# Graph network kernel: one wait per batch on GpSimd, on a TensorE product, in all three edge passes

## The chip, the cores and the metric

The kernel runs on one core of one Trainium2 chip. The metric is device time in microseconds of one execution. Before the change, three timed runs took 8580.19, 8585.12 and 8589.28 us; their median is 8585.12 us.

## The reference, cut to what matters

Four graph layers run one after the other on 6250 nodes of 64 features and 206250 edges that are sorted by destination. After each, the node features are a layer norm of the old ones plus the layer's result.

```
L0 (mlp):   m = relu([x[src], x[dst], edge_attr_32] @ W1 + b1) @ W2 + b2 ; segment_sum(m, dst)
L1 (gatv2): g = leaky_relu(xl[src] + xr[dst] + edge_attr_16 @ W_e) ; logits = sum(g * att)
            softmax over the edges of one destination, out = segment_sum(alpha * xl[src]) ...
L2 (gat):   e = leaky_relu(s_src[src] + s_tgt[dst]) ; softmax ; segment_sum(attention * h[src])
L3 (mean):  segment_sum(x[src]) / counts
```

The first three gather a row of a node table for every edge (`x[src]`, `xl[src]`, `h[src]`). This gather is what the change touches.

## The kernel before, in words

L0, L1 and L2 are each run by `edge_pass` (L195), followed by a `dense` stage; L3 is a function of its own. The pass of L0 is called mlp, that of L1 gatv (in the program gatv2), that of L2 gat. gatv and gat are the *soft* passes, those with a softmax (`soft`, L197).

A pass walks over 231 batches (`NB`) of 7 tiles (`B`) of 128 edges. Each engine has its own program of steps, one per batch, and the programs are tied together by counting semaphores; `b.used(k)` is n + 1 - k for batch n, so `wait(eng, sem, b.used(k))` waits until batch n - k has passed the place that counts `sem`. A wait for a count of zero or less is not issued at all (`wait`, L138). SyncE, VectorE, ScalarE and TensorE run their steps in a loop with eight batches in its body and the first and last batches written out (`over_batches`, L144); GpSimd's program has all 231 batches written out.

What each engine does for a batch n:

- **GpSimd** (L459 to L473) waits, then issues 7 indirect DMAs (L470), one per tile, which gather 128 rows each from the node table into slot n mod 8 of the tile `G` (8 slots, `GQ`). It computes nothing else in this part of the pass.
- **SyncE** loads the edge's relative destinations (`rel`, L361), edge attributes (L367), 4 of the 7 windows of the destination table (L374 and L167 through `load_windows`) two batches ahead, and stores results. ScalarE's queue loads the other 3 windows.
- **VectorE** makes one-hot matrices of the destinations for the next batch (`one_hots`, L489), adds the gathered rows to TensorE's product z (`add_gathered`, L510, counting `z_added`), makes the matrix of equal destinations (L496) and, in the soft passes, the prefix maxima (L526, L530), the difference from the maximum of the batch two behind (L547, which waits for TensorE's turned maxima, `max_turned`) and the weighted messages (L554, counting `msg_ready`).
- **ScalarE** applies the nonlinearity to z plus the gathered rows (L717 or L713), exponentials, copies sums and the "build" blocks out of PSUM (L705, L734).
- **TensorE**, in this order in a step i: the first group of a build block (L865), `make_z(i + 1)` (L794 to L813, counting `z_made`), in the soft passes `turn_max` and `turn_logits` (L821, L828), the sums by destination (L846), in mlp the degree counts (L855), and the second group of the build block. `make_z(b)` itself waits for `z_added` of batch b - 2 in mlp, and for `act_done` of b - 2 and `msg_ready` of b - 3 in the soft passes, so that only two z tiles in PSUM are in use.

What holds GpSimd back before the change:

- In mlp: `z_added` of batch n - 8, that is, the slot of `G` is free again. GpSimd runs eight batches ahead.
- In the soft passes two waits: `msg_ready` of batch n - 8 (the slot is free), and `z_made` of batch n - 1, which keeps GpSimd no more than about one batch ahead. `msg_ready` is a count of VectorE's, `z_made` one of TensorE's. For the first eight batches of a soft pass the wait for `msg_ready` would be for a count of zero or less and is not there.

Of the kernel before, what the change touches and what calls it, by code (L numbers as in the profile page):

```python
# [32 lines left out]
GQ = 8  # L33
# [104 lines left out]
def wait(eng, sem, count):  # L138

    if not isinstance(count, int) or count > 0:  # L140
        eng.wait_ge(sem, count)
# [53 lines left out]
def edge_pass(nc, L, S, hist):  # L195

    soft = L.heads > 0  # L197
# [6 lines left out]
    with ctx:  # L204
# [6 lines left out]
        def sem(name):  # L211
            return ctx.enter_context(nc.semaphore(f"{L.name}_{name}"))
# [84 lines left out]
        sums_made = sem("sums_made")  # L297
        sums_copied = sem("sums_copied")
        z_added = sem("z_added")
        act_done = sem("act_done")  # L300
        if L.window:
            win_in = [sem(f"win_in{q}") for q in range(Q)]
            hot_made = sem("hot_made")
            z_made = sem("z_made")
        if ax:
            attr_in = [sem(f"attr_in{q}") for q in range(Q)]
        if soft:
# [10 lines left out]
            msg_ready = sem("msg_ready")  # L318
# [37 lines left out]
        def _(sp):  # L356
# [54 lines left out]
            def load_steps(n):  # L411

                for h, (k, m) in enumerate(THIRDS):
                    if n == LOAD_AT[h]:
                        sp.wait_ge(step_stored, 16)
                        if h:
                            sp.wait_ge(tiles_hot, h)
                            sp.wait_ge(groups_made, k)
                        sp.dma_start(tile_of[:, 0:m, :].rearrange("p b e -> p (b e)"),
                                     S["step_of"][k * P:(k + m) * P].unsqueeze(0).to_broadcast([P, m * P])  # L420
                                     ).then_inc(tiles_in, 16)
                    g = (n - LOAD_AT[h]) * LOADS
                    w = min(LOADS, m - g)
                    if g >= 0 and w > 0:
                        _, firsts = nc.values_load_multi_w_load_instructions(
                            first_tile[0:1, k + g:k + g + w], engines=[sp.engine], min_val=0, max_val=NTP - P,
                            skip_runtime_bounds_check_because="the least of a tile's number and the last window's")
                        for j, first in enumerate(firsts):
                            sp.dma_start(step_rows[:, g + j, :], S["tile_rows"][bass.ds(first, P), :]
                                         ).then_inc(rows_in, 16)  # L430
# [26 lines left out]

        @block.gpsimd
        def _(pool):  # L459
            freed = {"mlp": z_added, "gatv2": None, "gat": None, "mean": sums_made}[L.name]  # L460
            freed = freed or msg_ready

            for n in range(NB):
                b = Batch(0, n)
                wait(pool, freed, b.used(GQ))
                if soft:
                    wait(pool, z_made, b.used(1))
                for j in range(b.tiles()):
                    t = n * B + j
                    pool.indirect_dma_start(  # L470
                        out=G[:, b.gq, j * L.gathered:(j + 1) * L.gathered], out_offset=None, in_=L.gather_table,
                        in_offset=bass.IndirectOffsetOnAxis(ap=S["src_cols"][:, t:t + 1], axis=0)
                    ).then_inc(gathered[b.gq], 16)  # L473
            pool.wait_ge(written, 16 * (4 + 2 * HEADS * hist))
            for r in range(RA):
                pool.wait_ge(back_copied, sum(1 for _, first, _ in backs if first <= r))
                pool.indirect_dma_start(
                    out=S["C_" + L.name], out_offset=bass.IndirectOffsetOnAxis(ap=S["carry_row"][:, r:r + 1], axis=0),
                    in_=carried_rows[:, r, :], in_offset=None, bounds_check=NP - 1, oob_is_err=False
                ).then_inc(S["scattered"], 16)  # L480
            pool.wait_ge(S["scattered"], 16 * (RB * L.index + RA))

        @block.vector
        def _(dve):
# [118 lines left out]
            def carry_tails(n):  # L603
                v, through = nc.vector, S["through"]
                if soft and n == turns_at:
                    dve.wait_ge(tails_in, 16 * len(PASS_TAILS))
                    for c, (_, k) in enumerate(PASS_TAILS):
                        last = widen(v, L, wide[0:k, c, :, :], tails[0:k, c, :, :])
                    last.then_inc(wide_made, 1)
# [91 lines left out]
        def _(act):  # L701
# [36 lines left out]
            def copy_tails(n):  # L738
                if 0 <= n - turns_at < len(turns):
                    to, _, t0, k, j0, m = turns[n - turns_at]  # L740
                    act.wait_ge(turned, n - turns_at + 1)
                    act.activation(to[:, t0:t0 + k * B].rearrange("f (n b) -> f b n", b=B)[:, j0:j0 + m, :],
                                   build_ps[0:M, 0:m * P].rearrange("f (b n) -> f b n", b=m)[:, :, 0:k], ACT.Copy
                                   ).then_inc(turns_copied, 1)
                if soft and n == scan_at + 1:
                    act.wait_ge(tops_shifted, 1)
                    act.activation(tail_max, tail_max, ACT.Exp)
                    act.activation(fade[:, 1:TA], fade[:, 1:TA], ACT.Exp).then_inc(faded, 1)
                if 0 <= n - backs_at < len(backs):
                    a, r, m = backs[n - backs_at]  # L750
                    act.wait_ge(back, n - backs_at + 1)
                    part, to = (slice(0, M), slice(0, M)) if a is state else (slice(D, M), slice(M, L.row))
                    act.activation(carried_rows[:, r:r + m, to],
                                   build_ps[:, 0:m * P].rearrange("p (r f) -> p r f", r=m)[:, :, part], ACT.Copy
                                   ).then_inc(back_copied, 1)
# [1532 lines left out]
```

## Time and profile before

| | |
|---|---|
| median of 3 runs | 8585.12 us (8580.19 to 8589.28) |
| the profiled execution's own time | 8576.33 us |
| its span in the trace | 8574.6 us |
| mean granted TensorE clock | 0.546 |
| TensorE matmuls busy | 5662.1 us (66% of the span) |
| TensorE weight loads busy | 4975.2 us (58%) |
| VectorE busy | 4808.3 us (56%) |
| ScalarE busy | 1444.1 us (17%) |
| GpSimd busy | 4949.5 us (58%) |
| gathers of the three passes (L470) | 1612 in each; first starts 87.4, 2889.4 and 5578.2 us, last starts 2671.7, 5367.0 and 8044.3 us |

Busy time counts an instruction from its start to its end on the engine; for a DMA issued by GpSimd that is the time that GpSimd works on it, not the transfer. Matmuls overlap, and their ends are modelled. Idle time is shown in front of the instruction that ended it, with what released it where the semaphores tell; "issue" means that nothing was waited for that the profile shows, "remote" that the releaser could not be named. A releaser that is a DMA of an earlier stage is a label without meaning, as the semaphores are used again in each pass. Busy shares are averages over stages; whether an engine sets the pace is read from who waits for whom within one batch.

### The profile page before, as it was taken

The numbers are of one execution on the slowest core, as the hardware profiler recorded it, in microseconds if no ns is written. First come the engines' busy times: TensorE is split into PE (matmuls) and PEld (weight loads), VectorE is DVE, ScalarE is ACT, GpSimd is POOL, SyncE is SP. The second block draws the span as 40 slices with busy tenths as digits, with TensorE's granted clock in tenths as the row PEclk, the third lists the DMA queues.
The fourth block names the chain that finished last, engine by engine and source line by source line (L and its number), as shares of the span: only waits on it lengthen the run. The fifth ranks groups of instructions, "written<-read, shape, count | busy, mean of one in ns | idle before, by whom it ended". The sixth has DMA issues, their size and how long they took to land. (4 is left out here: it accounts for less than half of the span.)

```text
span 8574.6 us, 134602 instructions
## 1 busy us (share of the span) xinstructions
PE 5662.1 (66%) x36891; PEld 4975.2 (58%) x36891; DVE 4808.3 (56%) x7961; ACT 1444.1 (17%) x4343; POOL 4949.5 (58%) x5209
## 2 busy tenths in 40 slices
PE   3666666666666666666666666367777777777469
PEld 2555555555555455555555555266666667666469
DVE  3344555555554566666666666455555555555355
ACT  1111111111111111111111111111111111111110
POOL 4555666666664466666666666366666666666534
PEclk6555555555555555555555555555555555555589
DMA  4644555555554444444444444344444444434377
GB/s 111 122 116 104 127 127 129 127 127 130 127 127 102 95 119 118 118 118 118 119 119 118 119 119 111 37 90 91 89 91 90 91 90 90 90 88 91 67 279 305
DMA packets 1384872, 995.21 MB, mean 116 GB/s; under 512 B 927343, under 2 KB 1293041, under 8 KB 1375058
## 3 DMA queue, kind: packets, MB, share of 16 engines
q1 hardware_dynamic: 906402, 750.00, 30.6%
q0 software_dynamic: 165856, 169.99, 12.5%
q10 hardware_dynamic: 312400, 72.71, 4.2%
q8 instruction: 92, 1.51, 0.1%
q14 instruction: 122, 1.00, 0.0%
HBM read 676.85 MB, written 315.92 MB: 116 GB/s over the span
## 5 line engine op out<-in xcount | busy, mean ns | idle before, releaser
L470 POOL DMA_INDIRECT mlp_G<-mlp_src,src_cols x1612 | 1531.2, 950 | 1096.4 <-DVE mlp_zs L510 626.0
L470 POOL DMA_INDIRECT gat_G<-gat_src,src_cols x1612 | 1529.2, 949 | 1036.1 <-issue 442.8
L470 POOL DMA_INDIRECT gatv_G<-gatv_src,src_cols x1612 | 1526.5, 947 | 1024.1 <-remote 491.8
L810 PE MATMUL gat_z<-gat_win,gat_hot 128*128 128x1 f32 x3234 | 719.1, 345 | 688.9 <-issue 415.5
L810 PEld LDWEIGHTS gat_z<-gat_win,gat_hot 128*128 128x128 f32 x3234 | 717.4, 328 | 716.1 <-issue 670.6
L806 PE MATMUL gatv_z<-attr_w,gatv_attrT 112*128 112x448 f32 x462 | 425.1, 1024 | 859.7 <-issue 663.6
L510 DVE TENSOR_TENSOR mlp_zs<-mlp_z,mlp_G 128x448 f32<-128x448 f32 x231 | 144.2, 624 | 1130.0 <-remote 843.2
L846 PE MATMUL gat_sums<-gat_msg,gat_same 128*128 128x65 f32 x3234 | 714.1, 410 | 5.2 <-issue 5.2
L846 PEld LDWEIGHTS gat_sums<-gat_msg,gat_same 128*128 128x128 f32 x3234 | 708.8, 330 | 5.3 <-issue 5.3
L846 PE MATMUL gatv_sums<-gatv_msg,gatv_same 128*128 128x68 f32 x3234 | 691.9, 403 | 4.6 <-issue 4.4
L846 PEld LDWEIGHTS gatv_sums<-gatv_msg,gatv_same 128*128 128x128 f32 x3234 | 689.2, 321 | 5.1 <-issue 5.1
L846 PE MATMUL mlp_sums<-mlp_act_out,mlp_same 128*128 128x64 f32 x3234 | 643.5, 377 | 33.1 <-issue 33.1
L806 PEld LDWEIGHTS gatv_z<-attr_w,gatv_attrT 112*128 112x128 f32 x462 | 115.7, 311 | 909.6 <-issue 909.0
L846 PEld LDWEIGHTS mlp_sums<-mlp_act_out,mlp_same 128*128 128x128 f32 x3234 | 614.8, 289 | 34.8 <-issue 34.6
L806 PE MATMUL mlp_z<-attr_w,mlp_attrT 128*128 128x256 f32 (+1 forms) x924 | 499.0, 642 | 188.9 <-issue 147.4
L865 PE MATMUL mlp_build_ps<-mlp_build_area 128*128 128x98 bf16 x1512 | 220.6, 267 | 562.6 <-ACT mlp_build_area L734 367.1
L640 DVE TENSOR_TENSOR gat_build_area<-gat_in_psum,src_lo 128x1280 bf16<-128x1280 bf16 x216 | 317.2, 1468 | 379.0 <-remote 370.0
L865 PEld LDWEIGHTS mlp_build_ps<-mlp_build_area 128*128 128x128 bf16 x1512 | 117.1, 122 | 659.6 <-ACT mlp_build_area L734 415.0
L547 DVE TENSOR_TENSOR gatv_diff<-gatv_logits,gatv_z 128x28 f32<-128x28 f32 x231 | 42.2, 183 | 780.1 <-DMA tile_rows<-prep_tile_rows 771.9
L810 PEld LDWEIGHTS mlp_z<-mlp_win,mlp_hot 128*128 128x128 bf16 x4851 | 347.0, 134 | 218.0 <-issue 196.1
L713 ACT ACTIVATE gatv_zs<-gatv_z 128x448 f32<-128x448 f32 x231 | 125.4, 543 | 1987.0 <-DVE gatv_z L510 1936.8
L810 PEld LDWEIGHTS gatv_z<-gatv_win,gatv_hot 128*128 128x128 bf16 x4851 | 303.8, 134 | 232.3 <-issue 232.3
(494 smaller groups left out, 10597.7 us busy)
## 6 DMA issues: line engine op xcount, KB each, us to landing
mean_block<-blocks SPq DMA_DIRECT2D x74, 1568.0 KB
sums_gatv<-gatv_out_rows SPq DMA_DIRECT2D x231, 252.0 KB
sums_gat<-gat_out_rows SPq DMA_DIRECT2D x231, 231.0 KB
blocks<-gat_build_area SPq DMA_DIRECT2D x216, 245.0 KB
mlp_rel<-rel_rows SPq DMA_DIRECT2D x231, 224.0 KB
sums_mlp<-mlp_out_rows SPq DMA_DIRECT2D x231, 224.0 KB
gatv_rel<-rel_rows SPq DMA_DIRECT2D x231, 224.0 KB
gat_rel<-rel_rows SPq DMA_DIRECT2D x231, 224.0 KB
```

The costliest lines, as they stand in the source:

```text
L470: pool.indirect_dma_start(out=G[:, b.gq, j * L.gathered:(j + 1) * L.gathered], out_offset=None, in_=L.gather_table, in_offset=bass.Indirec ...
L510: nc.vector.tensor_tensor(total.rearrange("p (b w) -> p b w", w=w), made.rearrange("p (b w) -> p b w", w=w), Gv[:, b.gq, :, L.gathered - w ...
L547: nc.vector.tensor_tensor(diff[:, b.q, :], logits[:, b.q, :], max_in[(b.q + 1) % 2][:, 0:B * H], ALU.subtract).then_inc(diff_ready, 1)
L640: nc.vector.tensor_tensor(hot_src[:, b.c % 2, :, :], bc(iota_of, 1, [P, per_batch, P]), bc(S["src_lo"][:, cols], 2, [P, per_batch, P]), AL ...
L713: act.activation(zs[:, b.q, :], z[b.q % 2][:, 0:B * L.window], ACT.Relu, scale=-1.0).then_inc(below_made, 1)
L806: pe.matmul(z[b.q % 2][:, t0 * w:(t0 + nt) * w], attrT[0:nt * ax, b.q, g, :], S["attr_w"][ax][0:nt * ax, 0:nt * w], start=True, stop=True)
L810: last = pe.matmul(z[b.q % 2][:, j * w:(j + 1) * w], hot[:, b.q, j, :], win[:, b.q, j, part * w:(part + 1) * w], start=not ax and part == ...
L846: last = pe.matmul(sums[b.q % 2][:, j * L.msg:(j + 1) * L.msg], same[:, b.q, j, :], rhs, start=True, stop=True)
L865: last = pe.matmul(build_in[g % len(build_in)][:, j * KEYS:(j + 1) * KEYS], hot_src[:, b.c % 2, k + j, :], hot_key[:, b.c % 2, k + j, :], ...
```

## The change

GpSimd's waits ahead of a batch's gathers are replaced by a single wait, for `z_made`: in the soft passes of batch n - 1 as before, without the wait for `msg_ready`; in mlp of batch n - 6 in place of `z_added` of batch n - 8. Nothing else in the program is different.

```
-            freed = {"mlp": z_added, "gatv2": None, "gat": None, "mean": sums_made}[L.name]
-            freed = freed or msg_ready
-
             for n in range(NB):
                 b = Batch(0, n)
-                wait(pool, freed, b.used(GQ))
-                if soft:
-                    wait(pool, z_made, b.used(1))
+                wait(pool, z_made, b.used(1 if soft else GQ - 2))
                 for j in range(b.tiles()):
                     t = n * B + j
                     pool.indirect_dma_start(
```

The slot stays safe without the waits that go: TensorE's z of batch n - 6 was itself made after `z_added` of batch n - 8, and in the soft passes z of batch n - 1 after `msg_ready` of batch n - 4.

## Rows read from the trace of the kernel before

**Rows 1.** The profile page: busy time by engine, and the costliest group.

```profile
PE 5662.1 (66%) x36891; PEld 4975.2 (58%) x36891; DVE 4808.3 (56%) x7961; ACT 1444.1 (17%) x4343; POOL 4949.5 (58%) x5209
...
L470 POOL DMA_INDIRECT mlp_G<-mlp_src,src_cols x1612 | 1531.2, 950 | 1096.4 <-DVE mlp_zs L510 626.0
```

**Rows 2.** GpSimd's waits in the whole trace: us in total, times, longest us.

```profile
POOL mlp_G L470 <- DVE mlp_zs L510: 626.0, 207, 12.3
POOL gatv_G L470 <- remote: 491.8, 220, 3.1
...
POOL gat_G L470 <- remote: 273.3, 116, 3.4
POOL gat_G L470 <- PE gat_z L810: 221.8, 69, 4.2
...
POOL gatv_G L470 <- PE gatv_z L810: 17.6, 8, 3.0
```

**Rows 3.** Timeline of one mlp batch: start us, us, engine, line, [idle before <-releaser].

```profile
1502.65 0.62 DVE L510 TENSOR_TENSOR mlp_zs<-mlp_z,mlp_G 128x448 f32<-128x448 f32 x1 [4.60 <-remote]
...
1503.55 0.94 POOL L470 DMA_INDIRECT mlp_G<-mlp_src,src_cols  x1 [2.45 <-DVE mlp_zs L510]
...
1504.76 0.59 PE L865 MATMUL mlp_build_ps<-mlp_build_area 128*128 128x98 bf16 x5 [1.96 <-ACT mlp_build_area L734]
...
1505.47 0.58 ACT L734 ACTIVATE mlp_build_area<-mlp_build_ps 128x490 bf16<-128x490 f32 x1 [0.76 <-PE mlp_build_ps L865]
...
1507.61 0.69 PE L810 MATMUL mlp_z<-mlp_win,mlp_hot 128*128 128x64 bf16 x9
...
1511.04 0.94 POOL L470 DMA_INDIRECT mlp_G<-mlp_src,src_cols  x1 [0.30 <-issue]
...
1512.14 0.42 PE L865 MATMUL mlp_build_ps<-mlp_build_area 128*128 128x98 bf16 x3
...
1513.53 0.62 DVE L510 TENSOR_TENSOR mlp_zs<-mlp_z,mlp_G 128x448 f32<-128x448 f32 x1 [4.59 <-remote]
```

**Rows 4.** Timeline of a gatv batch with a long gather run, and its neighbours.

```profile
4016.34 0.94 POOL L470 DMA_INDIRECT gatv_G<-gatv_src,src_cols  x1 [2.30 <-remote]
...
4027.02 0.94 POOL L470 DMA_INDIRECT gatv_G<-gatv_src,src_cols  x1 [2.24 <-remote]
4029.21 0.94 POOL L470 DMA_INDIRECT gatv_G<-gatv_src,src_cols  x1 [1.25 <-issue]
...
4035.45 0.94 POOL L470 DMA_INDIRECT gatv_G<-gatv_src,src_cols  x1 [0.30 <-issue]
...
4038.45 0.94 POOL L470 DMA_INDIRECT gatv_G<-gatv_src,src_cols  x1 [2.05 <-remote]
```

**Rows 5.** VectorE's adds (L510) after mlp's last gather, 2697 to 2746 us.

```profile
L510 DVE TENSOR_TENSOR mlp_zs<-mlp_z,mlp_G x5: 618/625/625, 2707.3 to 2732.6; 128x448 f32<-128x448 f32 x5
```

**Rows 6.** Timeline of gatv's batches 6 to 9, first gather of each and VectorE's L547.

```profile
2950.50 0.18 DVE L547 TENSOR_TENSOR gatv_diff<-gatv_logits,gatv_z 128x28 f32<-128x28 f32 x1 [1.82 <-DMA tile_rows<-prep_tile_rows]
2950.70 0.94 POOL L470 DMA_INDIRECT gatv_G<-gatv_src,src_cols  x1 [1.88 <-remote]
...
2961.03 0.94 POOL L470 DMA_INDIRECT gatv_G<-gatv_src,src_cols  x1 [1.90 <-remote]
...
2971.16 0.18 DVE L547 TENSOR_TENSOR gatv_diff<-gatv_logits,gatv_z 128x28 f32<-128x28 f32 x1 [1.73 <-DMA tile_rows<-prep_tile_rows]
2971.84 0.94 POOL L470 DMA_INDIRECT gatv_G<-gatv_src,src_cols  x1 [2.38 <-remote]
...
2982.54 0.94 POOL L470 DMA_INDIRECT gatv_G<-gatv_src,src_cols  x1 [2.28 <-remote]
```

**Rows 7.** GpSimd's separate wait instructions (line L141) in gatv: count, ns, first and last.

```profile
L141 POOLq EVENT_SEMAPHORE  x223: 17/17/17, 2971.1 to 5365.0; - x112
```

**Rows 8.** Timeline of gat: first gathers of two batches in a row.

```profile
7027.90 0.94 POOL L470 DMA_INDIRECT gat_G<-gat_src,src_cols  x1 [0.34 <-issue]
...
7039.01 0.94 POOL L470 DMA_INDIRECT gat_G<-gat_src,src_cols  x1 [3.93 <-PE gat_z L810]
```

## The prediction

> **What bounds the kernel now.** I began with the page. No engine is full: TensorE 66%, GpSimd 58%, VectorE 56% [rows 1]. Busy shares don't say what sets the pace, so I read one batch at a time in the timeline.
>
> In mlp a batch takes 10.88 us, from one add of gathered rows to the next (1502.65 to 1513.53) [rows 3]. The reader is to see two things there. TensorE's z matmuls end at 1508.30 (1507.61 + 0.69), and VectorE, which needs only z and rows gathered eight batches earlier, starts its add 5.2 us later, after 4.59 us idle. And GpSimd's seven gathers run from 1503.55 to 1511.98 (1511.04 + 0.94); the add starts 1.55 us after that. So z reaches its waiters not when its matmuls are done, but about 1.5 us after the last gather. I can't name the cause of this hold, and it could be a coincidence of phases; two places test it.
>
> The first is a gatv batch in which one gather came late: 1.25 us idle ahead of it instead of 0.30 [rows 4]. The run of seven then took 9.37 us (4027.02 to 4036.39), where the standard is 8.43. The next run started 11.43 us after this one (4038.45), against 10.68 for the batch in front (4016.34 to 4027.02). A gather run longer by 0.94 us makes the batch longer by 0.75. If GpSimd only followed a cycle of the other engines, its idle time would have taken this up, as it had 2.24 us of it. The second is the end of mlp, with no gathers left: five adds in 25.2 us, 6.3 us apart [rows 5]. That stage has no build blocks and is no fair rival, but it points the same way.
>
> So I read the steady cycle as a loop through GpSimd: z is released, GpSimd starts its gathers, 8.43 us of them (7 of 0.94 with 0.30 between), 1.5 us, next z released. In mlp: 0.90 + 8.43 + 1.55 = 10.88, which is the batch [rows 3]. Everything in the loop is fixed but the first term, the time from z to the first gather, and this is what the change edits.
>
> **The change, part by part.**
>
> *Soft passes, the wait for msg_ready goes.* It was never late (it asks for batch n - 8, while z of n - 1 implies n - 4), so it seems free. But two waits cost more than one. The trace holds both forms: the first eight batches of a soft pass have one wait, and the separate wait instruction appears 223 times in gatv, from 2971.1 on, batch 8 [rows 7]. With one wait the first gather starts 0.20 us after VectorE's L547 (2950.50 to 2950.70), which starts at the same release; with two, 0.68 us after it (2971.16 to 2971.84) [rows 6]. And the period follows: 10.33 us from batch 6 to 7 with one wait (2950.70 to 2961.03), 10.70 from 8 to 9 with two (2971.84 to 2982.54). The saving lies between 0.37 (periods) and 0.48 us (latency); I take 0.42, the middle. GpSimd really waited for z 220 + 8 times in gatv and 116 + 69 in gat [rows 2]: 413 x 0.42 = 173 us. In gat some batches don't wait (0.34 us of idle) and the next one waits longer (3.93 us) [rows 8]; the batches that don't wait count for nothing in this sum.
>
> The Trainium skill, Advanced Engine Details and Errata, section Miscellaneous Facts (Network/Comms), gives 50 to 100 ns for the reading of a semaphore by a sequencer. By that one wait fewer would be worth an estimated 41 us at most (413 x 0.1), and the sum of both parts 186; the trace shows four to five times as much, and I go by the trace.
>
> *mlp, z_added of n - 8 becomes z_made of n - 6.* The number of waits stays one. In the steady state the release moves within the same batch cycle: GpSimd now starts 0.28 us after the add's end (1503.27 to 1503.55); after the change it starts by the product that lets the add start, so it no longer waits through the add's 0.62 us. The nearest row for the new form is again the one-wait soft batch, 0.20 us after VectorE's start [rows 3, 6]: 0.90 - 0.20 = 0.70 us. Upper bound 0.70, lower bound 0.62 (0.90 - 0.28). 207 batches waited for the add [rows 2]: 207 x 0.70 = 145 us.
>
> What is queued behind GpSimd's wait: only its own gathers, and who waits for them is VectorE's add. It gathers six batches ahead instead of eight, still some 60 us before the add, so no add becomes late. Start of the pass: six batches instead of eight are gathered without a wait while windows still load; I price that at nothing, at worst two batches of gathers (17 us) moved, in either direction. No DMA, compute instruction or SyncE wait is added or moved in its queue; the gathers, 0.7 us earlier, meet the window loads at another phase, priced at nothing since TensorE waits for ScalarE and VectorE for z, not for a window, in [rows 3].
>
> *What is late next.* TensorE in mlp begins its batch 2.1 us after the add's start (1504.76, after ScalarE's copies) and its last build group starts at 1512.14 for 0.42 us and one more matmul of 0.24 [rows 3], about 10.3 us after the add's start. With a batch of 10.2 us the next start is at 12.3, so 2 us are left.
>
> **The sum.** 173 + 145 = 318 us. Made against the profiled execution: 8576 - 318 = 8258. The median of the runs lies 9 us above that execution (8585 against 8576), so 8267 us, 3.7% less.
>
> **The rivals.**
>
> *Half of it.* The soft passes gain only what a semaphore read costs, and the shift at batch 8 has another cause; or mlp doesn't follow, since in its first quarter batches are irregular. For: only a few one-wait batches stand in the trace. Against: both latency and period shift exactly at batch 8. The time: 145 + 41 = 186 us off gives 8399; only the soft part, 8412. The page named above stands behind the first form.
>
> *GpSimd only follows.* The pace is set by TensorE, VectorE and ScalarE together and the gathers come earlier into idle time. For: the constant 1.5 us is what any follower would show too. Against: the long run [rows 4]. Time 8585, within 0.2% of it.
>
> *Slower: the hold catches a product that now gets through.* In mlp the first build group's matmuls end at 1505.35, 1.80 us after the run of gathers starts, and ScalarE's copy follows at once at 1505.47 [rows 3]. This product is released although gathers run. With the run 0.70 us earlier it comes 2.5 us into it. If the hold begins between 1.8 and 2.5 us, the copy waits for the run's end, and TensorE's second group, the copies and the next batch's first group wait for it: 0.59 + 0.58 us and a group of matmuls of some 0.7, about 1.9 us in each of the 168 batches with build blocks, 319 us. With the soft gain kept: 8585 - 173 + 319 - 43 (mlp's 63 other batches at 0.70) = 8688. Against: in [rows 8] GpSimd did not wait at 7027.90, so that a z had been released during the run in front. The hold isn't strict and sets in late.
>
> *Nothing done.* The waits compile as before: not likely, as mlp already has a single one.
>
> **How the numbers follow.** Forecast 0.74, half of it 0.11, follower or nothing 0.04, slower 0.11. The forecast's own range: every batch gains the full bound, 231 x 0.70 + 446 x 0.48 = 376, so 8585 - 376 = 8209; lower bounds with a fifth of the batches lost, (207 x 0.62 + 413 x 0.37) x 0.8 = 225, so 8360. To hold 8 in 10 the range takes in the half case: 8209 to 8415. A measurement of this kernel tells 0.2%, 17 us, from no change: faster 0.85, same 0.04, slower 0.11.
>
> **What would show it.** GpSimd's separate wait instructions gone from the soft passes; its first gather 0.2 us after VectorE's L547 there and after the add's start in mlp; batches near 10.2 us in mlp and 10.3 in gatv; gather runs still 8.43 us with 0.94 each, and 1.5 us from their end to the add. Wrong, if the gap in front of a run grows by what was saved (follower), if the copy L734 of the first build group comes late (slower), or if single gathers stretch.

## The result, and the profile after

The changed kernel takes 8364.74 us (median of 4 runs, 8354.94 to 8372.41) beside 8582.66 us of the kernel before in the same comparison (4 runs, 8577.60 to 8589.28): ratio 0.9745, 95% interval 0.9728 to 0.9762, 218 us or 2.5% less. The forecast was 8267 with a range of 8209 to 8415: the sign and the loop through GpSimd held, the sum of 318 us was half as large again as what came.

The page of the changed kernel: the span, busy time, and the groups that answer to [rows 1].

```profile
span 8370.7 us, 134156 instructions
PE 5711.5 (68%) x36891; PEld 5016.8 (60%) x36891; DVE 4802.8 (57%) x7961; ACT 1501.3 (18%) x4343; POOL 4950.5 (59%) x5209
...
L465 POOL DMA_INDIRECT mlp_G<-mlp_src,src_cols x1612 | 1533.8, 952 | 1019.2 <-issue 425.1
L465 POOL DMA_INDIRECT gat_G<-gat_src,src_cols x1612 | 1526.5, 947 | 983.1 <-issue 422.4
L465 POOL DMA_INDIRECT gatv_G<-gatv_src,src_cols x1612 | 1526.4, 947 | 977.9 <-issue 421.4
...
L841 PE MATMUL mlp_sums<-mlp_act_out,mlp_same 128*128 128x64 f32 x3234 | 719.8, 378 | 281.9 <-issue 279.7
...
L484 DVE TENSOR_TENSOR gatv_hot<-gatv_rel,gatv_in_psum 128x896 bf16<-128x896 bf16 x231 | 250.8, 1086 | 659.6 <-DMA gatv_rel<-rel_rows 595.4
```

Busy time is the same within 50 us on every engine but ScalarE; the work didn't change, the idle time did. Idle time has moved: TensorE's sums in mlp stood idle 281.9 us (33.1 before), and VectorE's one-hots 659.6 us in gatv (4.7) and 728.0 in gat (14.9), while in gatv the idle time in front of its L547, now L542, fell from 780.1 to 82.3 us. The first and last gather of each pass show where the time went:

```profile
L465 POOL DMA_INDIRECT mlp_G<-mlp_src,src_cols x1612: 938/944/2809, 88.6 to 2597.1; - x180
L465 POOL DMA_INDIRECT gatv_G<-gatv_src,src_cols x1612: 938/944/3482, 2794.7 to 5224.7; - x180
L465 POOL DMA_INDIRECT gat_G<-gat_src,src_cols x1612: 938/944/2972, 5435.7 to 7847.3; - x180
```

Against the starts in the table of before, the gathers of mlp span 2508.5 us (2584.3 before), of gatv 2430.0 (2477.6), of gat 2411.6 (2466.1): 76, 48 and 54 us less. Between mlp's last gather and gatv's first lie 197.6 us (217.7 before), 20 less, where the last batches of mlp finish: GpSimd now runs six batches ahead instead of eight, so its last gather stands two batches nearer the end. The rest of the 204 us by which the spans differ is in the stages behind, 7 us. A single gather still takes 0.944 us.

GpSimd's waits in the whole trace, to stand beside [rows 2]: us in total, times, longest us.

```profile
POOL mlp_G L465 <- remote: 387.5, 193, 8.3
POOL gat_G L465 <- PE gat_z L805: 331.0, 157, 4.1
POOL gatv_G L465 <- PE gatv_z L805: 293.1, 132, 3.5
POOL gatv_G L465 <- remote: 190.2, 97, 3.1
...
POOL mlp_G L465 <- PE mlp_z L805: 163.1, 24, 12.4
...
POOL gat_G L465 <- remote: 132.7, 69, 2.9
```

The names of the releasers have turned over, and they are easily misread. The trace also records when a count was raised. "remote" stands where this was more than 1.5 us after the last matmul of z, "PE gatv_z" where it was less, and that can still be a held z:

```profile
3958.58 1.33 PE L805 MATMUL gatv_z<-gatv_win,gatv_hot 128*128 128x64 bf16 x21
...
3961.57 0.94 POOL L465 DMA_INDIRECT gatv_G<-gatv_src,src_cols  x1 [1.96 <-PE gatv_z L805]
```

Here z's matmuls ended at 3959.91, 1.66 us ahead of the gather. By the times of the counts, z was released as its matmuls ended (within 0.02 us), so really late by itself, in 80 of the 132 batches of gatv (2 before) and in 39 of the 157 of gat (43 before). So TensorE itself is what GpSimd waits for in about a third of gatv's batches, and in gat no more often than before.

GpSimd's idle time between the gathers of a run has changed too, before and after:

```profile
POOL gatv_G L470 <- issue: 442.5, 1383, 1.3
...
POOL gatv_G L465 <- issue: 421.4, 1382, 0.3
```

With the two waits of before, every tenth batch (16, 26, 36 and so on, 22 in gatv, and 9 batches of gat) had up to 1.25 us between its first and second gather instead of 0.30. The long run of [rows 4] is one of them. Now none has.

The separate wait instruction of [rows 7] is gone: of 447 on GpSimd (L141) one is left, outside the gathers.

```profile
L141 POOLq EVENT_SEMAPHORE  x1: 17/17/17, 8022.4 to 8022.4; - x1
```

One mlp batch, two lines of the kernel before that [rows 3] leaves out and then the changed kernel:

```profile
1508.11 3.23 PE L846 MATMUL mlp_sums<-mlp_act_out,mlp_same 128*128 128x64 f32 x14
...
1513.45 0.24 PE L865 MATMUL mlp_build_ps<-mlp_build_area 128*128 128x98 bf16 x1 [0.89 <-issue]
```

```profile
1502.29 1.95 PE L841 MATMUL mlp_sums<-mlp_act_out,mlp_same 128*128 128x64 f32 x8
...
1504.08 0.94 POOL L465 DMA_INDIRECT mlp_G<-mlp_src,src_cols  x1 [0.30 <-issue]
...
1505.18 0.27 PE L841 MATMUL mlp_sums<-mlp_act_out,mlp_same 128*128 128x64 f32 x1 [0.94 <-issue]
...
1506.59 1.13 PE L841 MATMUL mlp_sums<-mlp_act_out,mlp_same 128*128 128x64 f32 x5 [1.15 <-issue]
...
1506.97 0.62 DVE L505 TENSOR_TENSOR mlp_zs<-mlp_z,mlp_G 128x448 f32<-128x448 f32 x1 [4.17 <-remote]
1507.12 0.94 POOL L465 DMA_INDIRECT mlp_G<-mlp_src,src_cols  x1 [2.09 <-remote]
...
1510.53 0.59 PE L860 MATMUL mlp_build_ps<-mlp_build_area 128*128 128x98 bf16 x5 [1.49 <-issue]
```

GpSimd starts 0.15 us after the add begins (0.90 before): the edit did what it was to do, by slightly more than the 0.70 us forecast. But the run of gathers ended at 1505.02 (1504.08 + 0.94) and the add starts 1.95 us after it, where it was 1.55. TensorE's fourteen sums now straddle that point: eight run, one comes alone, five follow at 1506.59. Before, all fourteen and the degree counts lay ahead of it, and only a build matmul waited there (1513.45, 1.47 us behind the run). The first build group then starts 3.56 us after the add (1510.53 - 1506.97), 2.11 before.

And the soft passes, at the place of [rows 4]:

```profile
4003.71 0.94 POOL L465 DMA_INDIRECT gatv_G<-gatv_src,src_cols  x1 [2.26 <-PE gatv_z L805]
...
4007.36 1.09 DVE L484 TENSOR_TENSOR gatv_hot<-gatv_rel,gatv_in_psum 128x896 bf16<-128x896 bf16 x1 [3.97 <-DMA gatv_rel<-rel_rows]
...
4008.36 0.18 DVE L542 TENSOR_TENSOR gatv_diff<-gatv_logits,gatv_z 128x28 f32<-128x28 f32 x1
...
4010.74 0.60 DVE L549 TENSOR_TENSOR gatv_msg<-gatv_G,gatv_z 128x448 f32<-128x448 f32 x1
...
4011.21 0.94 POOL L465 DMA_INDIRECT gatv_G<-gatv_src,src_cols  x1 [0.30 <-issue]
...
4013.22 1.33 PE L805 MATMUL gatv_z<-gatv_win,gatv_hot 128*128 128x64 bf16 x21
...
4014.83 0.94 POOL L465 DMA_INDIRECT gatv_G<-gatv_src,src_cols  x1 [2.68 <-PE gatv_z L805]
```

The run of gathers ends at 4012.15. z's matmuls end at 4014.55 (13.22 + 1.33), GpSimd follows 0.28 us later. This z was late by itself: VectorE's one-hots waited for the rel load until 4007.36, its messages (L549, which TensorE's next z needs) came at 4010.74, and z after them.

### The profile page after: what moved, and what is told of

It reads as the page before. It is cut to its first block and busy times, and to the rows that moved or that the text cites. A ratio compares the mean times of both kernels' runs of the same rounds, so it can differ in the third digit from the quotient of the medians.

```text
span 8370.7 us, 134156 instructions
## 1 busy us (share of the span) xinstructions
PE 5711.5 (68%) x36891; PEld 5016.8 (60%) x36891; DVE 4802.8 (57%) x7961; ACT 1501.3 (18%) x4343; POOL 4950.5 (59%) x5209
## 5 line engine op out<-in xcount | busy, mean ns | idle before, releaser
L841 PE MATMUL mlp_sums<-mlp_act_out,mlp_same 128*128 128x64 f32 x3234 | 719.8, 378 | 281.9 <-issue 279.7
L841 PEld LDWEIGHTS mlp_sums<-mlp_act_out,mlp_same 128*128 128x128 f32 x3234 | 662.1, 292 | 305.8 <-issue 302.8
L484 DVE TENSOR_TENSOR gat_hot<-gat_rel,gat_in_psum 128x896 f32<-128x896 bf16 x231 | 250.5, 1084 | 728.0 <-DMA gat_rel<-rel_rows 678.1
L484 DVE TENSOR_TENSOR gatv_hot<-gatv_rel,gatv_in_psum 128x896 bf16<-128x896 bf16 x231 | 250.8, 1086 | 659.6 <-DMA gatv_rel<-rel_rows 595.4
L729 ACT ACTIVATE gat_build_area<-gat_build_ps 128x490 bf16<-128x490 f32 x432 | 248.6, 577 | 958.4 <-remote 648.9
L805 PE MATMUL mlp_z<-mlp_win,mlp_hot 128*128 128x64 bf16 x4851 | 352.9, 241 | 44.7 <-issue 44.7
```

The source lines that it names most:

```text
L484: nc.vector.tensor_tensor(hot[:, b.q, :, :], relv[:, b.q, :, :], bc(lane_of, 2, [P, B, P]), ALU.is_equal).then_inc(hot_made, 1)
L729: act.activation(block_out[:, b.c % 2, k * KEYS:(k + m) * KEYS], build_in[g % len(build_in)][:, 0:m * KEYS], ACT.Copy).then_inc(blocks_cop ...
L805: last = pe.matmul(z[b.q % 2][:, j * w:(j + 1) * w], hot[:, b.q, j, :], win[:, b.q, j, part * w:(part + 1) * w], start=not ax and part == ...
L841: last = pe.matmul(sums[b.q % 2][:, j * L.msg:(j + 1) * L.msg], same[:, b.q, j, :], rhs, start=True, stop=True)
```

## The experiments

The kernel before ran beside every group of experiments on the same chip, and its time differs from chip to chip: 8662.76 us (8 runs) on that of the first group, 7186.74 (7) on that of the second, 8568.51 (7) on that of the third, 7149.28 (7) on that of the fourth. So ratios are compared between groups, and microseconds only within one. Of the four groups, the second alone had the changed kernel itself beside it. Each kernel has one trace: the gathers of mlp, with the same program, span 2624.0 us in soft_only and 2607.2 in swapped, so differences under some 20 us between two traces say little. "Period" is the median distance of the first gathers of successive batches, batches 60 to 215 of a pass, read from the trace.

**First group: each half alone, and which of the two waits costs.**

```
soft_only:  if soft: wait(pool, z_made, b.used(1))   else: wait(pool, freed, b.used(GQ))
mlp_only:   if soft: both waits as before            else: wait(pool, z_made, b.used(GQ - 2))
swapped:    the kernel before; in the soft passes z_made is waited for first, msg_ready second
```

> The soft half of the change alone: in gatv and gat the wait for msg_ready goes, mlp keeps its wait for z_added of batch n - 8. Theory A (each pass is a loop through GpSimd's gathers, and each half shortens the time from z to the first gather in its own passes): the gathers of gatv and gat took 48 and 54 us less in the changed kernel, mlp's keep their old 2584 us; total about 8583 - 110 = 8475 us. Rival B (the passes follow TensorE and the others; the gain comes from somewhere in mlp alone, for instance fewer gathers ahead at its start): about 8583.

> The mlp half alone: one wait for z_made of batch n - 6 in mlp, the soft passes keep both waits. Theory A: mlp's gathers 76 us shorter as in the changed kernel, and some 20 us less between the last gather of mlp and the first of gatv; gatv and gat as before (2478 and 2466 us); total about 8583 - 105 = 8478 us, so that the two halves add up to the whole. Rival B: nothing like a sum, one of the halves makes all of the 218 us.

> The kernel before with the order of GpSimd's two waits turned round in the soft passes, still two waits. Theory A1 (what costs is that the late wait, for z, stands in an instruction of its own ahead of the DMA): if z now stands on the DMA itself and msg_ready in the separate instruction, the first gather comes 0.2 us after L547 instead of 0.68, and the time is that of the soft half alone, about 8475 us. Rival A2 (a second wait costs its time wherever it stands): about 8583 us, first gather still 0.6 to 0.7 us after L547.

soft_only: 8579.26 us, ratio 0.9898 (0.9882 to 0.9915), 84 us less. mlp_only: 8617.83 us, ratio 0.9946 (0.9914 to 0.9979), 45 us less, its five runs spread from 8573 to 8653. The expectations of 110 and 105 us were too high, and whether the two halves add up to the whole can't be said here, as the changed kernel wasn't run on this chip. In mlp_only the soft passes have the old form: gathers of gatv 2503.5 us and of gat 2503.1, against 2472.5 and 2459.9 in soft_only, 31 and 43 us less. Both halves gain, and both gain less than their term (173 and 145).

swapped keeps both waits and gains the same: 8579.52 us, ratio 0.9906 (0.9890 to 0.9923), gathers of gatv 2478.0 and of gat 2456.0 us. GpSimd's waits at L141 and a gather of it:

```profile
L141 POOLq EVENT_SEMAPHORE  x447: 17/17/17, 2973.8 to 8226.2; - x149
```

```profile
4003.84 0.94 POOL L470 DMA_INDIRECT gatv_G<-gatv_src,src_cols  x1 [2.03 <-PE gatv_z L810]
```

All 447 separate wait instructions are still there, and cost nothing that the times show. In the source order of before, the late wait (z_made) is the one with its own instruction and the wait that is never late rides on the DMA; swapped turns this round. So the soft half of the gain is not a wait saved, but the late wait moved onto the instruction that it holds back. This is shown: the two kernels differ from the kernel before in the order or the number of waits and in nothing else. Both also lose the long gap in every tenth run (mlp_only still has it in 22 batches of gatv and 20 of gat). Why a late wait in an instruction of its own costs 0.48 us more, and what makes the gap, is open.

**A pause in front of the gathers.** To ask whether the start of the gathers is what counts, the changed kernel got a filler of about the length of what had been saved, between the wait and the first gather.

```
                 wait(pool, z_made, b.used(1 if soft else GQ - 2))
+                pool.memset(idle[:, :], 0.0).then_inc(idled, 1)
                 for j in range(b.tiles()):
+                    if j == 1:
+                        pool.wait_ge(idled, n + 1)
```

> The changed kernel with a GpSimd memset of 128x512 between the wait and the seven gathers of each batch (some 0.5 us), and a satisfied wait for it ahead of the second gather. Theory A (loop through GpSimd): every batch is longer by about the memset and what it takes to issue, 0.6 to 0.9 us, in some 620 batches: 8365 + 370 to 560, that is 8735 to 8925 us. Rival B (GpSimd follows; there are 2.0 us of idle ahead of each run of gathers): 8365, at most 8400.

8577.72 us, ratio 0.9900 (0.9884 to 0.9917). A gatv batch of it:

```profile
4014.25 0.94 POOL L469 DMA_INDIRECT gatv_G<-gatv_src,src_cols  x1 [0.30 <-issue]
4016.91 0.52 POOL L464 MEMSET gatv_idle<- 128x512 f32 x1 [1.72 <-remote]
4016.93 0.18 DVE L546 TENSOR_TENSOR gatv_diff<-gatv_logits,gatv_z 128x28 f32<-128x28 f32 x1 [3.69 <-remote]
4017.59 0.95 POOL L469 DMA_INDIRECT gatv_G<-gatv_src,src_cols  x1 [0.15 <-issue]
```

This is the clearest view of the loop: the run ends at 4015.19, 1.72 us later GpSimd's filler and VectorE's L546 start within 0.02 us of each other, and 0.66 us after that the next gathers. The period is 10.81 us, which is 8.43 + 1.72 + 0.66, and the same as that of the two-wait form in mlp_only (10.81). The late start explains the old soft period whatever delays it.

But neither theory foretold the time. The pause moves the start by 0.46 us, and the median period of gatv is 10.81 us against 10.59 in soft_only, so it costs 0.22 a batch. In mlp, with the first gather 0.89, 0.70 and 0.24 us behind the add (soft_only, pause_before, mlp_only), the periods are 10.98, 10.80 and 10.61 us: the first 0.19 us of an earlier start brought 0.18, the next 0.46 only 0.19, as the time from the run's end to the add went from 1.66 and 1.67 to 1.94 us. The three passes' gathers span 57 us more than in the halves without the pause (soft_only's gatv and gat, mlp_only's mlp), where theory A had 370 to 560 us and theory B at most 35. The loop through GpSimd is there, but an earlier start is paid back in part only. The pass of mlp as a whole gains nothing from the last 0.46 us (2567.0 us with the pause, 2572.6 in mlp_only), since in 74 batches of mlp_only z is late by itself.

**Second group: repeat, a filler behind the gathers, an earlier rel load, fewer gathers.**

```
after_again:   the changed kernel
busy_after:    the same memset behind a batch's seven gathers
rel_early:     SyncE's load of rel (L361) for batch i + 3 in place of i + 2
five_gathers:  for j in range(min(B if n < GQ else 5, b.tiles()))
               (leaves out two tiles' neighbours in every batch from the ninth on)
```

> The changed kernel once more, beside the runs of this call, as the yardstick for them. On the first chip it was 218 us (2.55%) faster than the kernel before. Expected: 0.970 to 0.980 of the kernel before on this chip too.

> The changed kernel with a GpSimd memset of 128x512 (some 0.5 us) behind the seven gathers of each batch, ahead of the wait. Theory C1 (z is held until the gathers' transfers have landed; what GpSimd itself does then is of no account): the memset lies in the 2.0 us of idle ahead of the next run, the time is that of the changed kernel, at most 20 us more for the waits. Theory C2 (z is held while GpSimd is at work): every release comes 0.5 us later, some 300 us more.

> The changed kernel with SyncE's load of the relative destinations one batch earlier. In the changed kernel VectorE's one-hots of gatv wait 3.3 to 4 us for this load, which is new. Theory D1 (with the shorter loop through GpSimd a second loop binds in the soft passes, through this load, which stands behind two stores and their waits in SyncE's queue): VectorE no longer waits for it, batches go to the 10.3 us that the first eight of a soft pass had, some 60 us off 8365, 0.7%. Rival D2 (the load is late because VectorE is early, and the loop through GpSimd still binds): no change within 0.2%.

> The changed kernel with five of seven gathers in every batch but the first eight; two tiles in seven then add the rows that an earlier batch left there. A run of gathers is 5.9 us instead of 8.4. Theory A (the loop through GpSimd sets the batch): 2.5 us less per batch until the next bound; with TensorE's 7 to 8 us of work per batch as the next, 1.5 to 2.5 us less in each of some 660 batches, 1000 to 1650 us off. Rival B (another loop sets it now): under 0.3 us per batch, under 200 us off.

On this chip nothing was as expected: the kernel before takes 7186.74 us, and the change gives 7137.17 us, ratio 0.9935 (0.9918 to 0.9952) and not 0.970 to 0.980. The reason stands in one mlp batch of after_again:

```profile
1503.92 0.69 PE L805 MATMUL mlp_z<-mlp_win,mlp_hot 128*128 128x64 bf16 x9
...
1504.42 2.20 PE L841 MATMUL mlp_sums<-mlp_act_out,mlp_same 128*128 128x64 f32 x14
...
1506.53 0.94 POOL L465 DMA_INDIRECT mlp_G<-mlp_src,src_cols  x1 [0.30 <-issue]
1507.78 0.94 POOL L465 DMA_INDIRECT mlp_G<-mlp_src,src_cols  x1 [0.31 <-issue]
1507.82 0.62 DVE L505 TENSOR_TENSOR mlp_zs<-mlp_z,mlp_G 128x448 f32<-128x448 f32 x1 [2.60 <-DMA mlp_G<-mlp_src,src_cols]
1509.02 0.95 POOL L465 DMA_INDIRECT mlp_G<-mlp_src,src_cols  x1 [0.30 <-issue]
```

No product is held while gathers run: the count of z is raised 0.01 us (median) after its last matmul in all three passes, where it was 5.22, 4.40 and 1.99 us in mlp, gatv and gat of the trace before. GpSimd never stops between batches (0.31 us), the period is 7 x 1.25 = 8.74 us, and VectorE waits for gathered rows. GpSimd's own work is the bound, and a shorter wait in front of it has little left to give. The filler behind the gathers then stands in the way: 7363.35 us, ratio 1.0246 (1.0229 to 1.0263), period 9.15 or 0.41 us more, 226 us over after_again or 0.34 us for each of 669 batches. rel_early: 7135.28 us, ratio 0.9932 (0.9915 to 0.9949), no change, and it could bring none here: the one-hots of gatv wait 4.9 us in all in after_again. Five gathers instead of seven: 6426.24 us, ratio 0.8943 (0.8926 to 0.8960), periods 7.03 us in mlp and 7.57 and 7.45 in gatv and gat, so two gathers less (2.5 us) give 1.7 and 1.2 to 1.3 us before others bind.

**Third group, on a chip that holds the products again: filler behind, and z of three batches back.**

```
busy_after_2:  as busy_after
three_back:    wait(pool, z_made, b.used(3 if soft else GQ - 2))
```

> The kernel with the memset behind the seven gathers again. On the chip of the call before, all kernels took some 1400 us less than on the first two chips: z was not held there and gathers ran one after another (0.30 us between batches), so that the 0.5 us stood in the way whatever theory holds. On a chip like that: again 2.5% over the kernel before. On a chip with the hold (kernel before at 8.58 to 8.66 ms): theory C1 (the hold ends when the gathers' transfers have landed): as the changed kernel, 0.975 to 0.98 of the kernel before, the memset is in the idle time. Theory C2 (z is held while GpSimd is at work): 0.5 us per batch more, 1.01 of the kernel before.

> The changed kernel with the soft passes' wait on z of batch n - 3 in place of n - 1: the same release once per batch, but the gathers are two batches further ahead. Theory E1 (only the moment in the cycle matters, not which batch is named): 0.975 of the kernel before on a chip with the hold, as the change; on a chip without the hold up to 0.5% less than the changed kernel, since the 148 waits for z that are left there (127 us) go. Theory E2 (being close behind z is what keeps the soft passes fast, since gathers far ahead meet other transfers or hold z for longer): slower than the changed kernel by over 0.5%.

busy_after_2: 8341.00 us, ratio 0.9735 (0.9719 to 0.9751), as without the filler. In its gatv pass:

```profile
4012.97 0.95 POOL L468 DMA_INDIRECT gatv_G<-gatv_src,src_cols  x1 [0.30 <-issue]
4013.91 0.54 POOL L472 MEMSET gatv_idle<- 128x512 f32 x1
4015.86 0.95 POOL L468 DMA_INDIRECT gatv_G<-gatv_src,src_cols  x1 [1.41 <-remote]
```

The filler takes 0.54 us of the 1.95 us between the runs and the next gather comes as before (period 10.43). So it is not GpSimd being busy that holds products back, and GpSimd isn't full there. Nor is it the landing of the gathers, which theory C1 named. In another batch of the same pass, the first gather and then GpSimd's DMA queue from 3931.97 to 3932.30 us (packets, MB, share):

```profile
3931.97 0.95 POOL L468 DMA_INDIRECT gatv_G<-gatv_src,src_cols  x1 [1.45 <-remote]
```

```profile
q0 software_dynamic: 9, 0.01, 7.2%
```

These nine packets belong to the run in front, whose last gather instruction ended at 3929.97 (a run's first packets start some 1.65 us after its first gather). In the median of this pass the last packet ends 1.14 us behind the run and z is released 0.6 us later, but where packets last until 2.2 us behind it, as here, z is released at 1.7 us all the same.

three_back: 8364.67 us, ratio 0.9760 (0.9743 to 0.9776), beside 0.9745 of the changed kernel in the first comparison. Within what these runs can tell, it makes no difference which product GpSimd waits for: whatever the count, it is released about 1.7 us behind the run.

**Fourth group: the two that the second left unanswered.**

> As five_gathers: the changed kernel, but from the ninth batch of a pass on only 5 of the 7 indirect gathers are issued (slots 5 and 6 keep old rows), so part of the neighbours' sum is left out. It is asked on a chip with the hold (kernel before 8.55 to 8.67 ms, products seen about 1.5 us after the last gather instruction). Theory A, the loop through GpSimd's run sets the batch there too (gathers, hold, add, release): two gathers fewer take 2 x 1.25 = 2.5 us off nearly every one of 669 batches, less what TensorE then lacks: 7.0 to 7.4 ms, ratio 0.81 to 0.86. Theory B, the hold is a fixed cadence or belongs to something other than the gathers (the scatters, TensorE's clock): under 1 us per batch, over 7.9 ms. On a chip without the hold (before 7.19 ms) it is to repeat 0.894.

> As rel_early: the changed kernel with SyncE's load of the rel rows issued three batches ahead instead of two, in the soft passes. It is asked on a chip with the hold. D1, the soft passes of the changed kernel are held back by a second loop through VectorE's one-hots, which wait for this load (659.6 us of idle time on the page of after): periods of 10.44 and 10.37 us come down towards 10.30, that is 40 to 60 us, ratio to the kernel before 0.967 to 0.970. D2, the one-hots have slack and the waits at them are only passed on: same as the changed kernel, ratio 0.9735 to 0.976.

This chip too holds nothing (before 7149.28 us), so neither question got its answer. five_2: 6353.69 us, ratio 0.8898 (0.8877 to 0.8919), as five_gathers. rel_early_2: 7116.91 us, ratio 0.9952 (0.9935 to 0.9968), with no gain over the changed kernel's 0.9935 on the other chip of this kind.

## Why the prediction came out as it did

*What held.* GpSimd's wait sets the start of the gathers, and the release of the next product follows the end of their run, 8.43 us long as forecast. One wait instead of two brings the start of a soft batch 0.2 us behind the release, and pause_before shows the old period of gatv come back with the old delay. That msg_ready was never late, and that its wait cost all the same, stands by swapped. The Trainium skill's 50 to 100 ns for a semaphore read (Advanced Engine Details and Errata, Miscellaneous Facts (Network/Comms)) would have given 41 us for the soft half; the gathers of gatv and gat lost 102 us here. The figure is no measure for this case, as swapped shows: it isn't a read that was saved.

*The step that failed* is the sentence "Everything in the loop is fixed but the first term". Both terms of the sum were priced one to one by it, and both were too large.

- The soft term, 173 us, measured 102 (48 + 54), and 29 of these come from inside the runs (442 to 421 us between gathers in gatv, 429 to 421 in gat): the long gap in every tenth batch went. The forecast read one such batch as a gather that came late, and did not count what removing it would bring. In front of the runs gatv gained only 26 us. A batch of gatv labelled "remote" waits 1.96 us now (190.2 over 97), 2.24 before (491.8 over 220): 0.28 us less, not 0.42. Of that 1.96 some 0.20 is the new start, so the time from the run's end to the release is 1.76 us, where it was 1.56 (2.24 - 0.68). And 80 batches wait 2.38 us on average for a z that is really late, where 2 did. The forecast looked for what is late next in mlp alone. In gatv there was a second path almost as long, through VectorE and TensorE's next z, and once GpSimd starts earlier it sets about one batch in three. In the trace it begins at the one-hots that wait for SyncE's rel load. That this load is its cause is argued, not shown: loading it earlier changed nothing on two chips without the hold, where the one-hots hardly waited anyway, and on one with it this wasn't tried. The load may only have taken over the wait that stood in front of L547 before. In gat z is late no more often than before; GpSimd waits in 226 batches instead of 185, for 2.05 us (463.7 over 226) instead of 2.68 (495.1 over 185).
- The mlp term, 145 us, measured 96 (76 in the pass and 20 at its end), which is 0.42 us in each of 231 batches and not 0.70 in 207. The start moved by 0.75 us in the batch shown and 0.66 in the median, the period only from 10.88 to 10.46, since the time from the run's end to the add grew from 1.55 to 1.8 us in the median (1.95 in the batch shown). TensorE's matmuls resume 1.57 us behind the run (1506.59 - 1505.02), the add 0.38 us after them; before, it was 1.47 and 0.08. All of this moves TensorE's next batch back. The forecast saw 2 us left on TensorE, but counted them to the next start, not to the point at which its work is stopped as well. That the lag grows as the start comes earlier is shown on two chips; why it does is open.

*The rivals.* "Slower: the hold catches a product that now gets through" is near to what mlp shows, but what is caught are the sums, with nothing behind them that costs a whole group; it takes 0.3 us, not 1.9. "GpSimd only follows" was wrong for this chip, though the small price of the pause shows that GpSimd was not far from following; it fits five_gathers, where GpSimd waits for z in 227 batches of gatv. "Half of it", at 8399, lies 34 us from the result, but for another reason than it gave: both halves paid, each in part. (In the sum of the slower rival 63 x 0.70 is 44, not 43.)

*The range* held the result because it had been widened for the half case, in which one term fails. That both terms came out at 0.6 to 0.7 of their size was not foreseen, so it is luck in part.

## What to carry to other kernels

When an engine waits for two semaphores ahead of an instruction, look which wait is in an instruction of its own: if it is the one that comes late, turn the order or drop the other. A wait moved by d on a loop is worth d only up to the next loop; list the other paths of every pass with their slack before multiplying, and take a constant lag in a loop (here 1.55 us) as something that can grow. And measure on more than one chip if a wait has no cause that you can name.

## What was not expected of the hardware

On two chips the same kernels ran 1400 us faster (the kernel before at 7149 and 7187 us against 8569, 8583 and 8663), because TensorE's products reached the other engines at once, with gathers under way; in the other three comparisons, on at least two more chips, they came 1.55 to 1.8 us after the last gather of a run. VectorE's count `z_added` is raised 0.01 us (median) after the add in the trace before, so it isn't every engine's count that is late. As the ends of matmuls are modelled, the trace can't tell whether on these chips TensorE's work or only its count came late. The hold depends neither on which product is waited for (three_back) nor on what GpSimd does behind its gathers, nor does it end with the landing of the last packets (busy_after_2). What it is, and why some chips show it and others don't, is open; five gathers on a chip that has it would have been the next step. The value of this change hangs on it: 2.5% with the hold, 0.65% without.
